# VectorE's own-result waits: counted for each thread apart, placed at the reader, with other threads' operations allowed in between

## The reference

```
x = x + ga * L0_attn(h)   # 8 heads of 16, scores from Wq, Wk; the top 102 of 512 scores of each row
                          # get weight 1.24, a pooled and convolved column factor, softmax, Wv, Wo
x = x + gb * L0_ffn(h)    # norm, mix, norm, router softmax, top 2 of 8 experts, all computed densely
x = x + ga * L1_attn(h)   # Mamba: causal conv of 4, delta/B/C projections, scan over 512 steps, 16 states
x = x + gb * L1_ffn(h)    # top 2 of 8 experts with capacity 153: gather, silu(h * g), project, scatter back
```

## Time and profile before

| | |
|---|---|
| median of 3 runs | 3255.71 us (3254.84 to 3260.02) |
| the profiled execution: its own time | 3258.22 us |
| its span, first to last instruction | 3257.0 us |
| DVE busy | 2622.8 us, 81% of the span, 6653 instructions |
| PE busy / PEld busy | 2246.6 us, 69% / 1152.6 us, 35% |
| ACT busy / POOL busy | 1554.5 us, 48% / 1230.0 us, 38% |
| mean granted TensorE clock | 0.814 of full speed |

### The profile page before, as it was taken

How to read it: one execution, slowest core, us unless ns; L and a number is a source line. 1 busy time by engine, 2 the same in 40 slices (tenths; PEclk the granted TensorE clock), 3 DMA queues, 4 the chain that set the end, 5 groups by cost and what they waited for, 6 DMA issues and landing times.

```text
span 3257.0 us, 34429 instructions
## 1 busy us (share of the span) xinstructions
PE 2246.6 (69%) x8767; PEld 1152.6 (35%) x8767; DVE 2622.8 (81%) x6653; ACT 1554.5 (48%) x3348; POOL 1230.0 (38%) x1118
## 2 busy tenths in 40 slices
PE   4168296866758777777868668586868768658644
PEld 2015132543225432444225422244324433335213
DVE  5974888889889897889889898988989797954482
ACT  3306633664136743577246832467326752634322
POOL 1020063613435144532545144441636134533461
PEclk7578597887869889788979779797979789779757
DMA  3011012232122212223123211223122321313222
GB/s 96 0 29 27 0 46 78 77 78 59 47 71 81 80 52 65 88 63 98 53 77 82 83 49 55 70 71 95 49 71 82 74 76 40 101 36 110 74 68 90
DMA packets 137464, 215.15 MB, mean 66 GB/s; under 512 B 17872, under 2 KB 57440, under 8 KB 134112
## 3 DMA queue, kind: packets, MB, share of 16 engines
q1 hardware_dynamic: 133088, 203.88, 22.3%
q0 software_dynamic: 4096, 8.40, 0.9%
HBM read 190.06 MB, written 22.15 MB: 65 GB/s over the span
## 4 chain that ended last, share of the span: by engine, by line
DVE 40%; PE 27%; issue 16%; ACT 5%; POOL 5%; DMA 3%; DVEq 2%; SPq 1%; POOLq 0%; ACTq 0%
DVE wmask L763 12%; PE ps_att L1014 4%; PE ps_rest L1293 4%; PE ps_rest L1303 3%; DVE best L897 3%; DVE hg L1574 2%; PE ps_att L1025 2%; DVE hfc L1562 2%; PE ps_rest L1519 2%; DVEq L899 2%; DMA qk<-bounce 1%; POOL gat L1602 1%; PE ps_rest L1389 1%; DMA cols<-slots 1%; PE ps_att L842 1%
## 5 line engine op out<-in xcount | busy, mean ns | idle before, releaser
L763 DVE TENSOR_SCALAR_CACHE_REDUCE wmask<-z,tc 128x512 bf16<-128x512 f16 x640 | 439.2, 742 | 24.7 <-ACT z L730 21.8
L1328 ACT ACTIVATE sil<-ps_rest,w_b1T 128x512 f32<-128x512 f32 x256 | 175.6, 687 | 478.3 <-PE ps_rest L1303 448.4
L1363 POOL TENSOR_TENSOR gat<-sil,cbs 128x512 f32<-128x512 f32 x256 | 324.8, 1270 | 159.8 <-PE ps_rest L1293 101.9
L931 POOL TENSOR_SCALAR wmask<-wmask 128x512 bf16<-128x512 bf16 x256 | 161.1, 629 | 429.7 <-DVE wmask L888 419.4
L1014 PE MATMUL ps_att<-z,Vp 128*32 128x128 f32 x2048 | 283.6, 286 | 28.0 <-DVE z L1086 28.0
L1303 PE MATMUL ps_rest<-rest_hT,WF 128*128 128x512 f32 x512 | 286.5, 647 | 2.7 <-ACT sil L1328 2.7
L1615 POOL TENSOR_TENSOR rest_c<-rest_c,hg 128x512 f32<-128x512 f32 x128 | 162.2, 1267 | 327.8 <-DVE hg L1574 327.8
L696 PE MATMUL ps_att<-qk 128*128 128x512 bf16 x512 | 232.6, 475 | 67.1 <-DVE g_rank L879 29.8
L1293 PE MATMUL ps_rest<-gat,WP 128*128 128x512 f32 x512 | 272.9, 616 | 7.3 <-POOL gat L1363 6.7
L1014 PEld LDWEIGHTS ps_att<-z,Vp 128*32 128x32 f32 x2048 | 210.1, 114 | 137.3 <-issue 117.1
L1519 PE MATMUL ps_rest<-hg,ident 128*128 128x512 f32 x256 | 180.3, 794 | 112.1 <-DVE hg L1574 111.5
(11 more groups left out here) (361 smaller groups left out, 5101.7 us busy)
## 6 DMA issues: line engine op xcount, KB each, us to landing
cbs<-spreads SPq DMA_DIRECT2D x128, 256.0 KB, 3.7
ccs<-spreads SPq DMA_DIRECT2D x128, 256.0 KB, 3.4
WF<-in_w SPq DMA_DIRECT2D x64, 256.0 KB, 2.6
WP<-in_w SPq DMA_DIRECT2D x64, 256.0 KB, 2.7
WF<-in_wfc SPq DMA_DIRECT2D x64, 256.0 KB, 2.6
WG<-in_wgate SPq DMA_DIRECT2D x64, 256.0 KB, 3.0
WP<-in_wproj SPq DMA_DIRECT2D x64, 256.0 KB, 3.4
qk<-bounce SPq DMA_DIRECT2D x32, 384.0 KB, 5.5
```

Source lines behind the costliest of these rows:

```text
L763: od.up(dve.tensor_scalar(wmask[:, i, :], z_at[i], tc[:, 0, i:i + 1], None, ALU.is_ge, ALU.add, accum_out=tc[:, 1, i:i + 1]))
L1363: weighed0.up(pool.tensor_tensor(gat[m % 2], sil[m % 2], cbs[e % 2][:], ALU.mult))
```

## The change

Every VectorE thread gets an `Own` of its own: `o_setup`, `o_prep`, `o_att`, `o_pick`, `o_mix`, `o_rest`, `o_fin`. All still raise the one semaphore and share one running count, but each remembers the count of its own last operation, and its `settle` waits for that number alone. `settle` moves from behind the producer to ahead of the reader, with a yield between; the three helpers become generators that yield after each operation. So the planner may put operations of other threads between any two dependent ones. A yield may now give two numbers: how long VectorE is taken, and when the result is ready (mostly 0.12 us later). `weave` moves the engine's clock by the first and the thread by the second, and counts the second as work done. Some single costs are restated (a small operation 0.26 becomes 0.10, or 0.10 and 0.22). Attention's lead goes from 1.25 to 1.15 batches. No operation is added or removed, and no buffer changes.

```diff
 class Own:
-    def __init__(self, eng, sem):
-        self.eng, self.sem, self.n = eng, sem, 0
+    def __init__(self, eng, sem, count):
+        self.eng, self.sem, self.count, self.n = eng, sem, count, 0
     def up(self, ins):
         ins.then_inc(self.sem, 1)
-        self.n += 1
+        self.count[0] += 1
+        self.n = self.count[0]
         return self.n
...
-    od, oa = Own(dve, sem("dve")), Own(act, sem("act"))
+    s_dve, n_dve = sem("dve"), [0]
+    o_setup, o_prep, o_att, o_pick, o_mix, o_rest, o_fin = (Own(dve, s_dve, n_dve) for _ in range(7))
...
-    def dve_norm(w, b, k, src):
+    def dve_norm(o, w, b, k, src):
         for j in range(NT):
-            od.up(dve.bn_stats(w.stats[:, j, :], src[:, j, :]))
-            yield 0.26
-        od.settle()
+            o.up(dve.bn_stats(w.stats[:, j, :], src[:, j, :]))
+            yield 0.22 if j < NT - 1 else (0.22, 0.34)
+        o.settle()
...
-            od.up(dve.tensor_scalar(over, c, WIN_HI + 0.5, None, ALU.is_gt))
-            yield 0.26
+            o_att.up(dve.tensor_scalar(over, c, WIN_HI + 0.5, None, ALU.is_gt))
+            yield 0.10
...
-                od.up(dve.tensor_tensor(v["tn"], v["tn"], t, ALU.add)); od.settle()
-                yield 0.22
+                o_att.up(dve.tensor_tensor(v["tn"], v["tn"], t, ALU.add))
+                yield 0.10, 0.22
+                o_att.settle()
...
-    def dve_first_max(src, oh, vmax, scratch):
-        od.up(dve.tensor_reduce(vmax[:], src[:], AX.X, ALU.max)); od.settle()
-        od.up(dve.tensor_tensor(scratch[:], src[:], bcast(vmax), ALU.is_equal)); od.settle()
+    def dve_first_max(o, src, oh, vmax, scratch):
+        o.up(dve.tensor_reduce(vmax[:], src[:], AX.X, ALU.max))
+        yield 0.10, 0.22
+        o.settle()
+        o.up(dve.tensor_tensor(scratch[:], src[:], bcast(vmax), ALU.is_equal))
+        yield 0.10, 0.22
+        o.settle()
...
-            od.up(dve.scalar_tensor_tensor(z[:], xpad[k][:, 1:1 + S], cw[:, 1:2], a[:], ALU.mult, ALU.add)); od.settle()
-            yield 0.99
+            o_rest.up(dve.scalar_tensor_tensor(z[:], xpad[k][:, 1:1 + S], cw[:, 1:2], a[:], ALU.mult, ALU.add))
+            yield 0.87, 0.99
+            o_rest.settle()
...
-            elif isinstance(said, float):
+            elif isinstance(said, float) or isinstance(said[0], float):
+                busy, ready = (said, said) if isinstance(said, float) else said
                 needs.pop(t, None)
-                start += said
-                clock[name] = heads[t] = start
-                done[c] += said
+                clock[name] = start + busy
+                start += ready
+                heads[t] = start
+                done[c] += ready
...
-           (467.5, 1.25, (("pe", pe_choices()), ("act", act_choices()), ("dve", dve_choices()), ("pool", pool_choices()),
+           (467.5, 1.15, (("pe", pe_choices()), ("act", act_choices()), ("dve", dve_choices()), ("pool", pool_choices()),
```

More of the change, by code:

```diff
@@ L466, in pool_norm, with dve_split @@
         yield 1.06
[L468 to L472, removed]
+    def dve_split(o, src, dst, res, last):
+        o.up(dve.tensor_copy(dst[:, 0, :], src))
+        yield 0.35, 0.47
+        o.settle()
+        o.up(dve.tensor_tensor(res, src, dst[:, 0, :], ALU.subtract))
+        yield 0.62, 0.74
+        o.settle()
+        o.up(dve.tensor_copy(dst[:, 1, :], res))
+        yield 0.35, 0.47
+        o.settle()
         last.up(dve.tensor_tensor(dst[:, 2, :], res, dst[:, 1, :], ALU.subtract))
+        yield 0.62
     def sp_bounce(b, n, src, k):
@@ L622, in dve_rows @@
             dve.wait_ge(*counted.at(b - 1))
-        yield from dve_norm(att, b, 0, xr[b % 3])
+        yield from dve_norm(o_prep, att, b, 0, xr[b % 3])
     def dve_values(b):
@@ L805, in dve_search @@
+            o_att.up(dve.copy_predicated(t, over, v["tn"]))
+            yield 0.10, 0.22
+            o_att.settle()
             aim.up(dve.copy_predicated(t, under, v["tn"]))
-            yield 0.24
+            yield 0.10, 0.22
     xbank, sums = att.bank[0:3], att.bank[3]
@@ L965, in dve_rescale @@
         dve.wait_ge(*padded.at(b))
[L966 to L976, removed]
+        o_att.settle()
+        o_att.up(dve.tensor_scalar(c0[:], pool_pad[:, 0:S], cw[:, 0:1], wts["attn_cb"][:], ALU.mult, ALU.add))
+        yield 0.47, 0.59
+        o_att.settle()
+        o_att.up(dve.scalar_tensor_tensor(c1[:], pool_pad[:, 1:S + 1], cw[:, 1:2], c0[:], ALU.mult, ALU.add))
+        yield 0.67, 0.79
+        o_att.settle()
+        o_att.up(dve.scalar_tensor_tensor(c2[:], pool_pad[:, 2:S + 2], cw[:, 2:3], c1[:], ALU.mult, ALU.add))
+        yield 0.67, 0.79
+        o_att.settle()
+        o_att.up(dve.tensor_tensor(c1[:], KT[:], c2[:], ALU.mult))
+        yield 0.61, 0.73
+        o_att.settle()
+        yield from dve_split(o_att, c1[:], parts, c0[:], splitted)
     lbank, tbank, obank = att.bank[0], att.bank[2], att.bank[3]
@@ L1135, in dve_add, with dve_split_stacked @@
         yield 0.72
[L1137 to L1141, removed]
+    def dve_split_stacked(o, src, last):
+        o.up(dve.tensor_copy(cpart[:], src))
+        yield 0.58, 0.70
+        o.settle()
+        o.up(dve.tensor_tensor(cres[:], src, cpart[:], ALU.subtract))
+        yield 0.60, 0.72
+        o.settle()
+        o.up(dve.tensor_copy(cmid[:], cres[:]))
+        yield 0.33, 0.45
+        o.settle()
+        o.up(dve.tensor_copy(cpart[32:64], cmid[32:64]))
+        yield 0.20
         last.up(dve.tensor_tensor(cpart[64:96], cres[64:96], cmid[64:96], ALU.subtract))
+        yield 0.60
     def pe_spread(e, bank):
@@ L1239, in dve_mixture0 @@
         dve.wait_ge(*turned_back.at(b, 1))
-        yield from dve_norm(rest, b, 2, in_tiles(side))
+        yield from dve_norm(o_mix, rest, b, 2, in_tiles(side))
         yield lg_ps.at(b, 0)
         dve.wait_ge(*lg_ps.at(b, 0))
-        od.up(dve.tensor_reduce(sv["m"][:], logits0, AX.X, ALU.max)); od.settle()
-        yield 0.23
+        o_mix.up(dve.tensor_reduce(sv["m"][:], logits0, AX.X, ALU.max))
+        yield 0.10, 0.22
+        o_mix.settle()
         expl.up(dve.tensor_tensor(sm["t"][:], logits0, bcast(sv["m"]), ALU.subtract))
@@ L1270, in dve_mixture0 @@
         dve.wait_ge(*stack_ps.at(b, 0))
-        dve_split_stacked(side[0:96, :], stacks)
-        yield 2.20
+        yield from dve_split_stacked(o_mix, side[0:96, :], stacks)
     def pe_experts0(b):
@@ L1443, in dve_mamba @@
         dve.wait_ge(*added.at(b, 0))
-        yield from dve_norm(rest, b, 3, xr[b % 3])
+        yield from dve_norm(o_rest, rest, b, 3, xr[b % 3])
         for k in range(DC):
@@ L1696, in dve_mixture1 @@
         dve.wait_ge(*routed.at(b, 0))
-        od.up(dve.tensor_copy(goes[:], slot[:])); od.settle()
-        yield 0.21
+        o_rest.up(dve.tensor_copy(goes[:], slot[:]))
+        yield 0.10, 0.22
+        o_rest.settle()
         routed.up(dve.copy_predicated(goes[:], beyond[:], spare[:]))
@@ L1843, in dve_finish @@
             if i == 0:
-                od.settle()
+                o_fin.settle()
     def pool_finish(b):
```

296 lines of the change are left out of this document (165 added, 131 removed).

## The result

The changed kernel takes 3317.7 us against 3255.3 us: ratio 1.0193, 95% interval [1.0178, 1.0208]. It is 62 us slower where 40 us faster was forecast, and the time lies outside the stated range.

What follows compares the result with a forecast made beforehand. VectorE was taken as most loaded, not saturated: 87% busy while both chains run. Span 3257.0 - 40 from filled waits, other parts 0, gives 3217; with small corrections 3215 us, 8-in-10 range 3160 to 3285.

Steps and rivals of the forecast that it cites:

- the lead: Attention standing 0.10 batch less far ahead of rest: -16 us or about as much the other way; 0 taken.
- The margin: Last batch's attention ends at 2896.1, tokens before it turned at 2928.9: `mixture0`'s input waits some 33 us.
- the 36 us of the prediction: Shift of attention against rest expected from 0.10 batch less lead.
- sign for a collision elsewhere: If the new order collides away from these waits, only some batches' periods would change; no size given.
- The price of a wait: On VectorE, each wait for an own result costs 0.11 to 0.13 us, small or large; 0.12 taken.
- what the filled waits are worth: With both chains running, 670 of 838 VectorE waits filled at 0.12 us: 80 us of VectorE's time, bounds 50 and 100.
- the rule weighed in the prediction: VectorE's next operation doesn't start until the pipe is empty; by it the waits' sum would be zero.
- The share of 0.8: Share of VectorE's waits filled by another thread's operation with both chains running: between 0.5 and 1, 0.8 taken.
- 45 to 90: Fall of VectorE's busy time, in us, that the profile after would show if the prediction was right.
- half of it reaches the end: Of the 80 us of VectorE time freed, 40 us shorten the kernel, between estimates of 32 and 70.
- One reading behind it: The 330.9 us of VectorE waits are mostly on single TensorE results in choice and softmax, 44.4 and 43.1 us.
- The latency rival: Filled steps stretch small chains up to `mixture0`'s split, 0.77 us instead of 0.22: 3280 us; chance 0.23 with other slips.

Runs made afterwards that it cites:

- e1: The changed kernel with attention's lead put back from 1.15 to 1.25 batches, nothing else: 3253.5 us, ratio 1.0002.
- e9: The changed kernel (lead 1.15), same order, with the choice's mask operation on 128 of 512 columns: 3265.1 us, ratio 1.0029.
- e10: The changed kernel at a lead of 1.25, same order, with the choice's mask operation on 128 of 512 columns: 3215.3 us, ratio 0.9882.
- e4: The changed kernel (lead 1.15) with its planner told that VectorE is taken until the result is ready: 3330.6 us, ratio 1.0234.
- e7: The changed kernel at a lead of 1.25, planned as if VectorE were taken until the result is ready: 3243.6 us, ratio 0.9963.
- e12: The changed kernel at a lead of 1.25, with the overlap planned for rest's threads alone: 3261.7 us, ratio 1.0016.
- e11: The changed kernel at a lead of 1.25, with the overlap planned for attention's threads alone: 3244.2 us, ratio 0.9971.
- e3: The kernel before, same order, with each thread's own results counted apart and 43 waits moved behind their yield: 3245.7 us, ratio 0.9981.

## Why the prediction was wrong

**The step that failed is the lead.** It was taken as 0, with 16 us at most on either side, from one margin (2896.1 against 2928.9) and the thought that a shift uses it up. It measured 64 us in the changed planner and 127 in the old one. The margin was the wrong row. The shift was also smaller than the 36 us of the prediction: 0.10 batch moved the phase by 23 us (12.4 to 35.5). What the lead sets is which stages stand beside each other, for seven batches. Four windows of one period show it: the states of batch 2, then `mixture1` up to `tok`, then `mixture0` of batch 3, then its `experts0`. The columns are those of the earlier trace rows. At a lead of 1.25 (e1):

```profile
1306.30:1417.60 111.30, 83.37 (x466) 52.13 (x474) 106.05 (x180) 71.33 (x163) 68.86 (x48) 0.88 0.31 88
1417.60:1473.90 56.30, 26.89 (x101) 12.91 (x101) 43.51 (x156) 38.76 (x83) 11.19 (x12) 0.72 0.22 43
1473.90:1539.30 65.40, 44.79 (x241) 34.11 (x241) 62.34 (x216) 43.72 (x114) 9.68 (x10) 0.87 0.35 106
...
1539.30:1630.50 91.20, 86.23 (x221) 32.07 (x224) 78.73 (x187) 27.32 (x43) 57.93 (x59) 0.97 0.19 57
```

The changed kernel, at 1.15:

```profile
1294.60:1412.30 117.70, 79.17 (x327) 41.04 (x334) 110.91 (x185) 55.62 (x120) 78.37 (x55) 0.74 0.26 76
1412.30:1462.30 50.00, 41.71 (x250) 25.43 (x252) 32.60 (x120) 31.99 (x71) 11.15 (x12) 0.93 0.33 66
1462.30:1532.90 70.60, 48.04 (x252) 36.09 (x254) 55.52 (x185) 54.49 (x138) 9.69 (x10) 0.83 0.32 98
...
1532.90:1627.60 94.70, 77.89 (x184) 29.70 (x185) 85.20 (x234) 38.67 (x76) 50.83 (x48) 0.93 0.19 54
```

From one end of `experts0` to the next (1268.3 to 1630.5, and 1255.5 to 1627.6) this period is 9.9 us longer at 1.15: 6.4 in the states, 5.2 in `mixture0`, 3.5 in `experts0` and 1.1 in the mamba ahead of the first window, less 6.3 in `mixture1`. The reasons differ. In the states VectorE is busy for 110.9 us instead of 106.1: 7 of the choice's 32 tiles stand there, none at 1.25, and in exchange 21 instead of 32 operations of the softmax (line 1088). In the next two windows VectorE waits. It is idle for 5.3 + 12.8 + 3.1 = 21 us in the first three at 1.25, and for 6.8 + 17.4 + 15.1 = 39 us at 1.15. Over the whole span that comes to 44 us more idle time (699.1 against 3251.9 - 2596.8 = 655.1) and 19 us more busy time than in e1:

```profile
PE 2198.8 (68%) x8655; PEld 1145.9 (35%) x8767; DVE 2596.8 (80%) x6653; ACT 1554.5 (48%) x3348; POOL 1233.2 (38%) x1118
```

In the second window the end of attention's softmax, which waits on TensorE, now stands beside `mixture1`, which waits on everything; at 1.25 the search stood there, which is VectorE's own. These are some of VectorE's rows in that window at 1.15, with idle time in the brackets:

```profile
1417.23 0.69 DVE L1088 CUSTOM_DVE_ANT_0 z<-ps_att,wmask 128x512 f32<-128x512 f32 x1 [1.40 <-PE ps_att L1026]
1417.85 0.08 DVE L1088 DVE_READ_ACCUMULATOR2_ANT mx<- 128x1 f32 x1
1419.03 0.69 DVE L1088 CUSTOM_DVE_ANT_0 z<-ps_att,wmask 128x512 f32<-128x512 f32 x1 [1.09 <-PE ps_att L1026]
1419.64 0.08 DVE L1088 DVE_READ_ACCUMULATOR2_ANT mx<- 128x1 f32 x1
1420.34 0.75 DVE L1639 SCALAR_TENSOR_TENSOR rest_c<-cols,w_m_D,ps_rest 128x512 f32<-128x512 f32 x1 [0.61 <-PE ps_rest L1181]
```

In the third window the whole search stands beside `experts1` and `mixture0`, and with it the rounds in which ScalarE counts a share of the tiles (ScalarE busy 54.5 of 70.6 us against 43.7 of 65.4). VectorE waits there for ScalarE's part of `experts1`, 10.8 us in this window against 2.8 at 1.25. In the whole kernel it is 57.7 + 14.4 us before, 60.5 + 15.1 at 1.25 and 121.9 us now:

```profile
DVE hg L1887 <- ACT hfc L1846: 92.3, 67, 20.8
...
DVE gat L1887 <- ACT hfc L1846: 29.6, 34, 1.4
```

That these pairings are what costs is read from the traces; only the mask of the choice was tried by itself (e9, e10). The prediction's sign for a collision elsewhere, that only some batches' periods would change, didn't hold either: six of the seven are longer than before, by 8.2 to 17.4 us.

**The price of a wait was right, 0.12 us; what the filled waits are worth was not.** The changed kernel's router inside `mixture0`, where a search operation now stands between any two steps, as forecast:

```profile
1513.00 0.18 DVE L1190 TENSOR_TENSOR sm_t<-sm_p,sv_v 128x32 f32<-128x32 f32 x1
1513.11 0.74 DVE L773 TENSOR_SCALAR_CACHE_REDUCE wmask<-z,tc 128x512 bf16<-128x512 f16 x1
1513.77 0.08 DVE L773 DVE_READ_ACCUMULATOR wmask<-z,tc 128x1 f32 x1
1513.77 0.19 DVE L1193 TENSOR_TENSOR sm_t<-sm_t,iota_rev 128x32 f32<-128x32 f32 x1
1513.88 0.74 DVE L773 TENSOR_SCALAR_CACHE_REDUCE wmask<-z,tc 128x512 bf16<-128x512 f16 x1
1514.54 0.08 DVE L773 DVE_READ_ACCUMULATOR wmask<-z,tc 128x1 f32 x1
```

A step takes 0.77 us instead of 0.22, and VectorE loses only 0.10 to it. These rows agree with those of before, and not with the rule weighed in the prediction (the Trainium skill, VectorE: DVE Perf Modes, section The DRAIN you can't avoid). The same section adds that a next operation that is not held starts earlier, which the prediction left out and which the rows bear out. The share of 0.8 was too high at this lead: line 1193, the old 1156 of the earlier trace rows, had 1.1 us of idle time before it and has now

```profile
L1193 DVE TENSOR_TENSOR sm_t<-sm_t,iota_rev 128x32 f32<-128x32 f32 x32 | 6.1, 190 | 0.6
```

so about 0.6 / 0.034 = 18 of 32 still wait, and the starts give the same 18. Six of them stand where rest runs alone. Of the other 26, the 14 in `mixture0` are filled and the 12 in `mixture1` are not. At 1.25 it is 21 of the 26, 0.8 as forecast. Yet even there VectorE's busy time falls by only 26 us (2622.8 to 2596.8), where 45 to 90 were forecast, and none of it reaches the end: e1 is equal to the kernel before. The step "half of it reaches the end" measured 0. Why is open. One reading behind it was off: the waits of the choice and the softmax in the earlier trace rows are 87.5 of the 330.9 us, a quarter and not most, and all waits on TensorE together some 153 us.

**The latency rival** was put down as the way to become slower, with 65 us, all of it through `mixture0`. `mixture0` did become longer, but not by the fill. From the last start of `tok` to the end of the split, mean of batches 2 to 6, it takes 63.9 us before and 69.4 in the changed kernel, but 71.2 in e4, which plans no fill. At 1.25 it takes 64.1 us with the fill (e1) and 69.3 without (e7). TensorE's wait for `chosenT`, the last step of the router, went from 15.4 to 36.5 us, but its wait for the split fell from 26.0 to 7.7 us.

The stage that is longer with a fill is `mixture1`, from the last scan to `tok`, mean of batches 1 to 5: 45.4 us before, and at 1.25 56.1 and 56.2 with the fill in rest's chains (e1, e12) against 50.5 and 51.0 without (e7, e11). These 5 us a batch could be behind the 10 us between e1 and e7, but the shorter `mixture0` stands against them. No run takes them by themselves, and the planned orders of e1 and e7 differ elsewhere too, so that the 10 us are latency is not shown. At 1.15 the fill even gains 13 us (3330.6 to 3317.7). The sign of the result was covered by a case that is not the mechanism, and the size by none: that case ended at 3300 us.

**What held:** the tail is as before, within 5 us; waits by each thread's own number cost nothing (e3 gains 7.5 us). The first batch also comes forward by 17 us, and seven longer periods then take it back. That the prediction has a 16 us for the lead is a coincidence: it was half of the margin at the end, not an earlier start.

## What to carry to other kernels

When two long chains share engines in a fixed order, the constant that sets how far one runs ahead is not a tuning detail: it decides which stages stand side by side in every period. A step of 0.05 of a batch cost 18 to 86 us here, more than the 7.5 us that the own-result waits gave by themselves. What the traces suggest, and no run here proves, is to pair a stage that keeps the busiest engine full with one that waits on others. Read this from windows by stage, with busy and idle time, and not from the margin between the chains. And after any edit to planned costs, compare at equal phase before judging the edit.

## What was not expected of the hardware

Small VectorE operations that read two tensors took over 1 us in this kernel when the gating of `experts0` on GpSimd (line 1411) had started just before them:

```profile
1545.26 1.26 POOL L1411 TENSOR_TENSOR gat<-sil,cbs 128x512 f32<-128x512 f32 x1 [0.67 <-ACT cbs L1384]
1545.43 1.18 DVE L805 TENSOR_TENSOR d_tc<-lo_tc,hi_tc 128x64 f32<-128x64 f32 x1
```

The mean of this line is 465 ns where it was 286 as line 793, and 223 ns at a lead of 1.25:

```profile
L805 DVE TENSOR_TENSOR d_tc<-lo_tc,hi_tc 128x64 f32<-128x64 f32 x16 | 7.4, 465 | 0.8
```

Of its 16 operations, the 4 that start some 0.16 us behind one of GpSimd's last 1.18 us, and the other 12 last 0.23 us, also where GpSimd starts 0.18 us behind them. It counts as busy. The phase decides where it strikes: lines 805, 811, 814 and 820 of the search are busy for 40.2 us at 1.15 and for 15.9 at 1.25, while line 925 of the choice has 87.1 us at 1.15 and 102.1 at 1.25. Of line 925's 256 operations 46 last over 0.5 us at 1.15 and 60 at 1.25, and at the start of 42 and 53 of these a GpSimd tensor operation was running. All this was seen in the traces and not tried by itself. The Trainium skill, GPSIMD Engine Reference, section Specifications, says that GpSimd shares its SBUF interfaces with VectorE and contends with VectorE instructions that have two SBUF inputs (or run in a 2-port mode). The rows agree, and put the price at about 1 us (1.18 against 0.23) for an operation that is caught.
